# The projection stage with eight ticks of lead and TensorE's work in halves

## The chip, the core and the metric

The kernel runs on one core of one Trainium2 chip. TensorE multiplies matrices into PSUM, VectorE, ScalarE and GpSimd compute elementwise and scan, and SyncE issues every DMA here. The metric is the device time of one execution in microseconds, the median of several runs.

## What is computed

Four layers over a batch of four 64 x 64 images of 96 channels. The first two are state-space layers: group norm, an input projection to 2 x 192 channels, a depthwise convolution, then four scans (k = 0 to 3) over the 4096 pixels in four orders, with 16 states a channel. The change touches what follows a scan. In the reference's words, cut:

```
y = y1 + y2 + y3 + y4                      # the four directions; D * u is in them
mu, var = y.mean(-1), y.var(-1)            # over 192 channels
y = (y - mu) * rsqrt(var + 1e-05) * ln_w + ln_b
y = y * silu(z)
return y @ out_proj_w.T                    # 192 -> 96, added to x
```

Layers three and four are linear attention and a feed-forward network in a low-precision format, on the same images.

## The kernel before

**The scan.** Eight scans (4 images x 2 layers) of 16 windows of 24 steps, 3072 steps. In a step, TensorE fills two PSUM banks with B by a selection matmul (`fill`, L988), VectorE multiplies them by delta*u (L1501) and scans 128 x 1024 states (L1516); in two steps of eight GpSimd forms that product (L1601) and VectorE only scans (L1512). ScalarE gives the decay (L1255), GpSimd multiplies the states by C (L1593) and TensorE sums them (`reduce2`, L1001). `fill(n + 1)` waits for scan n - 1, since it writes over its bank. The loads of a window are SyncE's: a group of four 512 KB loads (`dtr`, `dur`, L697 and L702) at each of steps 0, 8 and 18, C and B (L682, L687) at steps 19, 21, 23 and 1.

**Side stages.** All else runs beside the scan as generators in `pre` (norm and convolution), `post` (sums, norm, gate, projection) and `attn`. Every engine steps its own copy twice a step: a tick. A window has 48 ticks, and a scan's first 15 windows have 720. A stage says at which tick each engine does what; engines wait for one another by semaphores alone. `LEAD` yields 14 ticks before the first stage of a scan, `X_LEAD` 8 ticks before a stage that loads x. The post of scan s runs in scan s + 1; the last one, post 7, has no scan beside it and runs in a tail with the last two attention layers.

**`post`.** It takes eight chunks of 512 pixels, the 192 channels as two halves h of 96. Beside a scan a chunk starts every 39 ticks (`POST_EVERY`), in the tail every 13 (`POST_LANES`); s is a chunk's own tick. TensorE sums four directions and D*u in PSUM at s = 0, 2, 4, 8, 10 (L836; the loads are `sd<-y_d` and `sd<-u_d`, the fourth and fifth given at s = 3 and 5), ScalarE copies (L1114), TensorE centres (L846, L847), ScalarE copies and squares (L1118, L1119), TensorE sums the squares (L852), ScalarE takes the root (L1122, L1124), VectorE multiplies (L1426), ScalarE applies weight and bias (L1128), GpSimd multiplies by z (L1559), TensorE projects (L857) and VectorE adds to x (L1431). In the tail VectorE forms the sum itself (L1412 to L1421), and three lanes of buffers let chunks overlap. An fp32 matmul stands in the profile as two records.

In layer 0 two of the four directions are read with a stride (8 floats in a row), in layer 1 all are contiguous. Posts 0, 1, 4, 5 are of layer 0; 2, 3, 6, 7 of layer 1.

Of the kernel before, what the change touches and what calls it, by code (L numbers as in the profile page):

```python
# [238 lines left out]
def build_program(nc, a, out):  # L239
# [17 lines left out]
    with ctx:  # L257
# [217 lines left out]

        def post_every(overlapped):
            return POST_EVERY if overlapped else POST_LANES
# [7 lines left out]
        def post_ticks(overlapped):  # L485
            return post_every(overlapped) * (C8 - 1) + 39
# [20 lines left out]
        def _(sp):  # L507
# [82 lines left out]
            def post(j, overlapped):  # L590
# [174 lines left out]
        def _(pe):  # L765
# [48 lines left out]
            def post(j, overlapped):  # L814
                b, l = order[j]
                done = before["post", j]
                side_banks(done)
                if not overlapped:
                    pe.wait_ge(scan_v, W * NT)
                for tick in range(post_ticks(overlapped)):  # L820
                    for c in range(C8):
                        s = tick - post_every(overlapped) * c
                        m = C8 * done.post + c
                        bank = lane(c, overlapped).bank
                        if overlapped and s in SUM_AT:
                            i = SUM_AT.index(s)
                            k = SUMS[i]
                            buf, arrived, n = sum_buffer(m, 5 * c + i, overlapped)
                            pe.wait_ge(arrived, n)
                            if i == 0:  # L830
                                after(pe, px_v, through(m, c, overlapped))
                            for h in range(2):
                                v = buf[:, h, :]
                                if l == 0 and k in (1, 3):
                                    v = v.rearrange("p (w r) -> p r w", r=ROWS)
                                mm = pe.matmul(ps[0:CH, bank + h, :], eye[:, :] if k < K else dg[:, l, h, :], v,  # L836
                                               start=(i == 0), stop=(i == K))
                            mm.then_inc(sm_p, 1)
                        if s == 15:
                            if overlapped:  # L840
                                pe.wait_ge(ys_a, m + 1)
                            else:
                                pe.wait_ge(yt_v, c + 1)
                                after(pe, px_v, through(m, c, overlapped))
                            for h in range(2):
                                pe.matmul(ps[0:CH, bank + h, :], cen[:, :], lane(c, overlapped).ys[:, h, :], start=True, stop=False)  # L846
                                mm = pe.matmul(ps[0:CH, bank + h, :], crs[:, :], lane(c, overlapped).ys[:, 1 - h, :], start=False, stop=True)  # L847
                            mm.then_inc(ct_p, 1)
                        if s == 20:
                            pe.wait_ge(xc_a, m + 1)  # L850
                            for h in range(2):
                                mm = pe.matmul(ps[0:CH, bank, :], o192[:, :], lane(c, overlapped).zq[:, h, :], start=(h == 0), stop=(h == 1))  # L852
                            mm.then_inc(pv_p, 1)
                        if s == 35:
                            pe.wait_ge(pg_g, m + 1)
                            for h in range(2):
                                mm = pe.matmul(ps[0:CH, bank + 1, :], wo[:, l, h, :], lane(c, overlapped).ys[:, h, :], start=(h == 0), stop=(h == 1))  # L857
                            mm.then_inc(pj_p, 1)
                    yield
# [196 lines left out]
        def _(act):  # L1056
# [46 lines left out]
            def post(j, overlapped):  # L1103
                b, l = order[j]
                N = before["post", j].post
                for tick in range(post_ticks(overlapped)):
                    for c in range(C8):
# [3 lines left out]
                        if overlapped and s == 12:  # L1111
# [3 lines left out]
                        if s == 17:  # L1115
# [4 lines left out]
                        if s == 22:  # L1120
# [4 lines left out]
                        if s == 26:  # L1125
# [212 lines left out]
        def _(dve):  # L1338
# [60 lines left out]
            def post(j, overlapped):  # L1399
                N = before["post", j].post  # L1400
                for tick in range(post_ticks(overlapped)):
                    for c in range(C8):
# [19 lines left out]
                        if s == 24:  # L1422
# [5 lines left out]
                        if s == 37:  # L1428
# [110 lines left out]
        def _(pool):  # L1539
# [10 lines left out]
            def post(j, overlapped):  # L1550
                N = before["post", j].post
                for tick in range(post_ticks(overlapped)):
                    for c in range(C8):
                        if tick - post_every(overlapped) * c == 27:
# [151 lines left out]
```

## Time and profile before

| | |
|---|---|
| median of 3 runs | 12069.41 us (12066.87 to 12089.06) |
| the profiled execution | 12060.41 us, its span 12058.5 us |
| TensorE, VectorE, ScalarE, GpSimd busy | 74%, 84%, 59%, 81% |
| mean granted TensorE clock | 0.726 of 2.4 GHz |
| DMA | 1630 MB, mean 135 GB/s |
| issue to landing, `dtr`, `dur`, `sd<-y_d` (median) | 8.0, 8.6, 5.1 us |

The span is from the first to the last instruction. Busy time of an engine leaves out issuing and waiting. In the timeline a row is a run of equal instructions of one engine; what stands in brackets is the idle time of the engine just before it and who ended it. SPq is SyncE's queue: its time in a row is that of issuing, which grows when the queues are full.

### The profile page before, as it was taken

To read this page: it belongs to the slowest core of one execution; us is meant where nothing else is said; L and a number is where in the kernel's file an instruction comes from. 1 tells how busy PE (TensorE), PEld (TensorE's weight loads), DVE (VectorE), ACT (ScalarE), POOL (GpSimd) and SP (SyncE) were. 2 spreads that over 40 slices of the span, in tenths; PEclk is the share of its full clock that TensorE was granted. 3 is DMA by queue.
4 is the path that set the end of the run, shared out by engine and by line. 5 is a ranking of instruction groups with operands and counts; after the bars stand their busy time and mean duration, and the time that the engine had idled before them with its cause. 6 is when DMAs were issued, how large, how long until landed. Compare 5 with 4: busy or idle time off the path is not lost.

```text
span 12058.5 us, 94250 instructions
## 1 busy us (share of the span) xinstructions
PE 8904.7 (74%) x26272; PEld 2246.7 (19%) x26272; DVE 10157.8 (84%) x6020; ACT 7059.9 (59%) x10794; POOL 9743.3 (81%) x4231
## 2 busy tenths in 40 slices
PE   6876677876779667778777777787677976777746
PEld 2211111211112111212112121122111221121112
DVE  3899988899889988889888897898888888888841
ACT  4665555664556555576556765566655665557726
POOL 3799988888888988888888887888888888888830
PEclk8875566865779567778677776787677976777756
DMA  4666688566776566556675668766677656655530
GB/s 98 138 140 127 132 145 147 141 133 135 147 146 147 133 142 162 135 124 153 151 165 131 126 147 147 143 142 137 132 148 150 142 131 153 146 142 125 122 97 6
DMA packets 1781576, 1630.40 MB, mean 135 GB/s; under 512 B 1323950, under 2 KB 1325264, under 8 KB 1781052
## 3 DMA queue, kind: packets, MB, share of 16 engines
q1 hardware_dynamic: 1781052, 1624.37, 62.0%
q8 instruction: 212, 3.47, 0.1%
q14 instruction: 312, 2.56, 0.1%
HBM read 624.25 MB, written 194.51 MB: 68 GB/s over the span
## 4 chain that ended last, share of the span: by engine, by line
issue 24%; POOL 19%; DVE 19%; PE 19%; ACT 8%; SPq 6%; DMA 5%; DVEq 0%; POOLq 0%; ACTq 0%
POOL pr L1593 12%; DVE ps L1501 8%; DVE hs L1516 8%; POOL dur L1601 4%; PE ps L836 3%; PE ps L1001 3%; SPq L702 3%; PE ps L805 3%; POOL us L1584 2%; DVE hs L1512 2%; PE ps L988 2%; ACT dec L1255 2%; DMA sd<-y_d 1%; PE ps L963 1%; PE ps L979 1%
## 5 line engine op out<-in xcount | busy, mean ns | idle before, releaser
L1593 POOL TENSOR_TENSOR pr<-hs,crep 128x1024 f32<-128x1024 f32 x3072 | 7190.3, 2353 | 1506.3 <-DVE hs L1516 956.4
L1516 DVE TENSOR_TENSOR_SCAN hs<-dec,carry,ps 128x1024 f32<-128x1024 f32 x1728 | 4054.2, 2346 | 233.8 <-ACT dec L1255 10.3
L988 PE MATMUL ps<-sbc,selb 96*128 96x512 bf16 x4608 | 1859.3, 496 | 2013.1 <-DVE hs L1516 1292.4
L1501 DVE TENSOR_TENSOR ps<-ps,dur 128x1024 f32<-128x1024 f32 x2304 | 2788.6, 1210 | 556.2 <-PE ps L988 420.1
L1255 ACT ACTIVATE dec<-dtr,ac 128x1024 f32<-128x1024 f32 x2304 | 2611.2, 1136 | 372.1 <-DVE hs L1516 371.6
L1001 PE MATMUL ps<-pr,red 128*32 128x512 f32 x12288 | 2290.0, 828 | 79.7 <-POOL pr L1593 73.8
L1262 ACT ACTIVATE carry<-hs 128x1 f32<-128x1 f32 x2304 | 457.3, 199 | 2688.8 <-DVE hs L1516 2311.4
L1601 POOL TENSOR_TENSOR dur<-dur,brep 128x1024 f32<-128x1024 f32 x768 | 1805.9, 2351 | 124.1 <-DMA brep<-bc_d 110.4
L1512 DVE TENSOR_TENSOR_SCAN hs<-ps,carry,dur 128x1024 f32<-128x1024 f32 x576 | 1342.4, 2337 | 330.3 <-POOL dur L1601 247.9
L1516 DVE TENSOR_TENSOR_SCAN hs<-dec,zero,ps 128x1024 f32<-128x1024 f32 x576 | 1351.2, 2346 | 82.2 <-ACT dec L1255 11.0
L805 PE MATMUL ps<-xb,tapw 96*96 96x512 f32 x2304 | 1200.1, 643 | 37.9 <-ACT sd L1091 35.5
L988 PEld LDWEIGHTS ps<-sbc,selb 96*128 96x128 bf16 x4608 | 368.9, 108 | 4198.6 <-DVE hs L1516 2382.8
L1255 ACT ACTIVATE ps<-dtr,ac 128x1024 f32<-128x1024 f32 x768 | 848.3, 1105 | 390.2 <-DVE hs L1516 390.1
L979 PE MATMUL ps<-xdf,tapw 6*96 6x512 f32 x1024 | 770.9, 842 | 62.4 <-ACT sbc L1222 34.7
L963 PE MATMUL ps<-us,xp 96*102 96x512 f32 x1024 | 690.8, 812 | 107.1 <-ACT us L1208 77.9
L836 PE MATMUL ps<-sd,eye 96*96 96x512 f32 x896 | 646.5, 854 | 166.9 <-DMA sd<-y_d 166.8
L1584 POOL TENSOR_TENSOR us<-us,de 96x1024 f32<-96x1024 f32 x256 | 603.3, 2357 | 159.0 <-ACT de L1239 159.0
L1512 DVE TENSOR_TENSOR_SCAN hs<-ps,zero,dur 128x1024 f32<-128x1024 f32 x192 | 447.9, 2338 | 124.4 <-POOL dur L1601 112.9
L1001 PEld LDWEIGHTS ps<-pr,red 128*32 128x32 f32 x12288 | 277.6, 125 | 1235.3 <-issue 939.9
L805 PEld LDWEIGHTS ps<-xb,tapw 96*96 96x96 f32 x2304 | 359.0, 170 | 768.7 <-issue 692.9
L1222 ACT ACTIVATE sbc<-ps 96x512 bf16<-96x512 f32 x768 | 443.9, 578 | 23.1 <-PE ps L969 22.9
L1208 ACT ACTIVATE us<-ust 96x128 f32<-96x128 f32 (+3 forms) x608 | 350.1, 652 | 90.1 <-DMA ust<-u_d 90.1
(220 smaller groups left out, 6883.4 us busy)
## 6 DMA issues: line engine op xcount, KB each, us to landing
dtr<-de SPq DMA_DIRECT2D x768, 512.0 KB, 8.0
dur<-us SPq DMA_DIRECT2D x768, 512.0 KB, 8.6
crep<-bc_d SPq DMA_DIRECT2D x512, 512.0 KB, 5.4
ust<-u_d SPq DMA_DIRECT2D x256, 384.0 KB, 6.7
y_d<-yst SPq DMA_DIRECT2D x768, 128.0 KB, 4.4
sd<-y_d SPq DMA_DIRECT2D x448, 192.0 KB, 5.1
brep<-bc_d SPq DMA_DIRECT2D x128, 512.0 KB, 5.8
u_d<-sd SPq DMA_DIRECT2D x64, 384.0 KB, 3.1
```

Of the source, the lines that this page charges most:

```text
L805: mm = pe.matmul(bank, tap[:, l, t, h * CH:(h + 1) * CH], xb[:, c * ROWS + t // 3:c * ROWS + t // 3 + ROWS, t % 3:t % 3 + SIDE], start=(t ...
L836: mm = pe.matmul(ps[0:CH, bank + h, :], eye[:, :] if k < K else dg[:, l, h, :], v, start=(i == 0), stop=(i == K))
L979: pe.matmul(ps[0:CH, PB, :], dtw[:, order[s][1], k, h * CH:(h + 1) * CH], xdf[XD:XROWS, :], start=True, stop=True, tile_position=(XD, 0)). ...
L988: mm = pe.matmul(ps[:, SLOT + 2 * (n % RS) + hf, :], selb[:, i % GT // 2, :], sbc[:, w % 2, B * hf:B * (hf + 1)], start=True, stop=True)
L1001: mm = pe.matmul(ps[32 * strip:32 * strip + 32, YB, :], red[:, :], pr[:, (2 * m + j) % RP, B * hf:B * (hf + 1)], start=(q == 0), stop=(q = ...
L1255: act.activation(to, dtr[:, 2 * (G % 2) + i % 2, :], ACT.Exp, scale=ac[:, order[s][1], k, i:i + 1]).then_inc(exp_a, 1)
L1501: dve.tensor_tensor(slot(n), slot(n), dur[:, 2 * (G % 2) + i % 2, :], ALU.mult).then_inc(bu_v, 1)
L1512: dve.tensor_tensor_scan(hs[:, n % RH, :], slot(n), dur[:, 2 * (G % 2) + i % 2, :], init, ALU.mult, ALU.add).then_inc(scan_v, 1)
L1516: dve.tensor_tensor_scan(hs[:, n % RH, :], dec[:, others(n) % RD, :], slot(n), init, ALU.mult, ALU.add).then_inc(scan_v, 1)
L1584: pool.tensor_tensor(v, v, de[:, half(h, w), :], ALU.mult).then_inc(du_g, 1)
L1593: pool.tensor_tensor(pr[:, n % RP, :], hs[:, n % RH, :], crep[:, q, :], ALU.mult).then_inc(prod_g, 1)
L1601: pool.tensor_tensor(v, v, brep[:, :], ALU.mult).then_inc(bup_g, 1)
```

## The change

Beside a scan, `post` yields eight more ticks on every engine: SyncE after the first six half tiles of y and the load of x, the others before anything. TensorE's sums, which stood with both halves in one tick, stand in two following ticks; the centring in s = 15 and 17, the sum of squares in 21 and 22, the projection in 35 and 36. The other engines' ticks move by one or two. The ticks of the chunk also move in the tail, where there is no lead.

```diff
+        def post_lead(overlapped):
+            return X_LEAD if overlapped else 0
...
                 load_x(done, a["x"][b] if l == 0 else x_d[b])
+                for _ in range(post_lead(overlapped)):
+                    yield
...
-                        if s == 22:
+                        if s == 23:
                             sp.wait_ge(pv_p, m + 1)
...
-                        if overlapped and s in SUM_AT:
-                            i = SUM_AT.index(s)
+                        at = s - s % 2
+                        h = s % 2
+                        if overlapped and at in SUM_AT:
+                            i = SUM_AT.index(at)
...
-                            for h in range(2):
-                                v = buf[:, h, :]
...
-                            mm.then_inc(sm_p, 1)
-                        if s == 15:
...
+                            if h == 1:
+                                mm.then_inc(sm_p, 1)
+                        if s in (15, 17):
+                            h = (s - 15) // 2
+                            if h == 0 and overlapped:
                                 pe.wait_ge(ys_a, m + 1)
...
-                            for h in range(2):
-                                pe.matmul(ps[0:CH, bank + h, :], cen[:, :], lane(c, overlapped).ys[:, h, :], start=True, stop=False)
-                                mm = pe.matmul(ps[0:CH, bank + h, :], crs[:, :], lane(c, overlapped).ys[:, 1 - h, :], start=False, stop=True)
-                            mm.then_inc(ct_p, 1)
-                        if s == 20:
...
+                        if s in (21, 22):
+                            h = s - 21
...
-                        if s == 35:
...
+                        if s in (35, 36):
+                            h = s - 35
```

ScalarE's ticks 12, 17, 22, 26 become 13, 19, 24, 28; VectorE's 24 and 37 become 26 and 38; GpSimd's 27 becomes 29. SyncE's 3, 5, 12, 14, 31 and 38 and VectorE's 11 (the sums of the tail) stay.

VectorE in the tail, from behind its first sum: before. L1412, L1413, L1416 and L1421 are the sum of a chunk, L1426 the multiply, L1431 the residual.

```order
L1426 TENSOR_TENSOR sd<-sd,ps 96x512 x2
L1412 TENSOR_TENSOR dec<-dec,us 96x1024
L1413 TENSOR_TENSOR us<-us 96x1024
L1416 SCALAR_TENSOR_TENSOR hs<-hs,dsum,us 96x512 x2
L1421 TENSOR_TENSOR pr<-dec,hs 96x1024
L1431 TENSOR_TENSOR xb<-xb,ps 96x8x64
L1426 TENSOR_TENSOR pr<-pr,ps 96x512 x2
L1412 TENSOR_TENSOR hs<-hs 96x1024
L1413 TENSOR_TENSOR dec<-dec 96x1024
L1416 SCALAR_TENSOR_TENSOR dec<-dec,dsum 96x512 x2
L1421 TENSOR_TENSOR crep<-hs,dec 96x1024
L1431 TENSOR_TENSOR xb<-xb,ps 96x8x64
```

The same place after the change (L1431, L1432, L1435 and L1440 are the sum, L1445 the multiply, L1450 the residual):

```order
L1431 TENSOR_TENSOR dec<-dec,us 96x1024
L1432 TENSOR_TENSOR us<-us 96x1024
L1435 SCALAR_TENSOR_TENSOR hs<-hs,dsum,us 96x512 x2
L1440 TENSOR_TENSOR pr<-dec,hs 96x1024
L1445 TENSOR_TENSOR sd<-sd,ps 96x512 x2
L1431 TENSOR_TENSOR hs<-hs 96x1024
L1432 TENSOR_TENSOR dec<-dec 96x1024
L1435 SCALAR_TENSOR_TENSOR dec<-dec,dsum 96x512 x2
L1440 TENSOR_TENSOR crep<-hs,dec 96x1024
L1450 TENSOR_TENSOR xb<-xb,ps 96x8x64
L1445 TENSOR_TENSOR pr<-pr,ps 96x512 x2
L1431 TENSOR_TENSOR us<-us 96x1024
```

The sum of the next chunk stood behind the multiply of the chunk before it; now it stands ahead of the multiply, and ahead of the residual too where there is one.

TensorE in the tail, the centring of chunk 2 and what follows it: before. `cen` and `crs` are centring, `o` the sum of squares, `wo` the projection.

```order
L846 MATMUL ps<-pr,cen 96x512
L847 MATMUL ps<-pr,crs 96x512
L846 MATMUL ps<-pr,cen 96x512
L847 MATMUL ps<-pr,crs 96x512
L852 MATMUL ps<-pr,o 96x512 x2
L857 MATMUL ps<-sd,wo 96x512 x2
L846 MATMUL ps<-crep,cen 96x512
L847 MATMUL ps<-crep,crs 96x512
L846 MATMUL ps<-crep,cen 96x512
L847 MATMUL ps<-crep,crs 96x512
L852 MATMUL ps<-crep,o 96x512 x2
```

After the change (L856 and L857 centring, L864 the sum of squares, L871 the projection):

```order
L856 MATMUL ps<-pr,cen 96x512
L857 MATMUL ps<-pr,crs 96x512
L856 MATMUL ps<-pr,cen 96x512
L857 MATMUL ps<-pr,crs 96x512
L864 MATMUL ps<-pr,o 96x512
L871 MATMUL ps<-sd,wo 96x512
L864 MATMUL ps<-pr,o 96x512
L871 MATMUL ps<-sd,wo 96x512
L856 MATMUL ps<-crep,cen 96x512
L857 MATMUL ps<-crep,crs 96x512
L856 MATMUL ps<-crep,cen 96x512
```

Both halves of the squares stood ahead of the projection of the chunk before; now the two alternate, a half each.

TensorE beside the scan, the first chunk of post 0, from the end of its sums: before. `selb` are fills, `red` reductions, `xp`, `neg` and `xdf` the scan's preparation.

```order
L1001 MATMUL ps<-pr,red 32x512 x4
L836 MATMUL ps<-sd,dg 96x512 x2
L979 MATMUL ps<-xdf,tapw 96x512
L1001 MATMUL ps<-pr,red 32x512 x4
L846 MATMUL ps<-sd,cen 96x512
L847 MATMUL ps<-sd,crs 96x512
L846 MATMUL ps<-sd,cen 96x512
L847 MATMUL ps<-sd,crs 96x512
L988 MATMUL ps<-sbc,selb 128x512 x2
L979 MATMUL ps<-xdf,tapw 96x512
L988 MATMUL ps<-sbc,selb 128x512 x2
```

After the change, from the first half of the centring:

```order
L1003 MATMUL ps<-sbc,selb 128x512 x4
L1016 MATMUL ps<-pr,red 32x512 x4
L856 MATMUL ps<-sd,cen 96x512
L857 MATMUL ps<-sd,crs 96x512
L1003 MATMUL ps<-sbc,selb 128x512 x2
L856 MATMUL ps<-sd,cen 96x512
L857 MATMUL ps<-sd,crs 96x512
L1003 MATMUL ps<-sbc,selb 128x512 x2
L1016 MATMUL ps<-pr,red 32x512 x4
L978 MATMUL ps<-us,xp 102x512 x2
L864 MATMUL ps<-sd,o 96x512
```

The eight records of centring stood together between two fills; each half has its own place now, and so has each half of the squares.

SyncE's queue from the first loads of post 0: before. `dtr` and `dur` are group 2 of the window.

```order
L588 DMA sd<-y_d 96x64x8 x4
L588 DMA sd<-y_d 96x512 x2
L549 DMA xb<-in_x 96x64x64
L697 DMA dtr<-de 128x1x1024 x2
L702 DMA dur<-us 128x1x1024 x2
L588 DMA sd<-y_d 96x512 x2
L588 DMA sd<-u_d 96x512 x2
L677 DMA bc_d<-xdf 32x512
L710 DMA y_d<-yst 64x512 x2
```

After the change:

```order
L591 DMA sd<-y_d 96x64x8 x4
L591 DMA sd<-y_d 96x512 x2
L552 DMA xb<-in_x 96x64x64
L702 DMA dtr<-de 128x1x1024 x2
L707 DMA dur<-us 128x1x1024 x2
L682 DMA bc_d<-xdf 32x512
L715 DMA y_d<-yst 64x512 x2
L591 DMA sd<-y_d 96x512 x2
L591 DMA sd<-u_d 96x512 x2
```

The fourth and fifth load (the `y_d` and `u_d` pairs behind `dur`) stood ahead of the copy `bc_d` and the store of y; now they stand behind both.

## Rows read from the trace of the kernel before

**Rows 1.** The page's costliest groups, VectorE's scan and multiply: busy, mean ns, idle before, releaser.

```profile
L1516 DVE TENSOR_TENSOR_SCAN hs<-dec,carry,ps 128x1024 f32<-128x1024 f32 x1728 | 4054.2, 2346 | 233.8 <-ACT dec L1255 10.3
...
L1501 DVE TENSOR_TENSOR ps<-ps,dur 128x1024 f32<-128x1024 f32 x2304 | 2788.6, 1210 | 556.2 <-PE ps L988 420.1
```

**Rows 2.** Table by stretch: PE, PEld, DVE, ACT, POOL busy (x); PEclk, DMA share, GB/s.

```profile
2532.00:2892.00 360.00, 235.92 (x672) 38.76 (x664) 338.15 (x187) 189.11 (x269) 330.32 (x144) 0.54 0.66 135
11563.00:11755.00 192.00, 102.28 (x129) 31.52 (x130) 66.20 (x64) 37.42 (x48) 21.77 (x8) 0.63 0.36 94
```

**Rows 3.** Waits over the span: who, for whom, us, times, longest.

```profile
DVE ps L1501 <- PE ps L988: 420.1, 214, 12.2
...
PE ps L836 <- DMA sd<-y_d: 166.8, 32, 13.2
...
DVE xb L1431 <- PE ps L857: 133.7, 29, 15.1
```

**Rows 4.** Timeline of post 2, first chunk: start, us, engine, line, then idle before it.

```profile
4399.68 6.22 SPq L702 DMA_DIRECT2D dur<-us  x2
...
4412.49 3.73 PE L836 MATMUL ps<-sd,eye 96*96 96x512 f32 x4 [9.86 <-DMA sd<-y_d]
...
4417.11 1.23 DVE L1501 TENSOR_TENSOR ps<-ps,dur 128x1024 f32<-128x1024 f32 x1 [8.15 <-PE ps L988]
```

**Rows 5.** Groups of VectorE in the first chunk of post 0.

```profile
L1501 DVE TENSOR_TENSOR ps<-ps,dur 128x1024 f32<-128x1024 f32 x16 | 19.5, 1216 | 17.1 <-PE ps L988 17.1
```

**Rows 6.** Groups of VectorE in the first chunk of post 2.

```profile
L1501 DVE TENSOR_TENSOR ps<-ps,dur 128x1024 f32<-128x1024 f32 x16 | 19.4, 1211 | 9.0 <-PE ps L988 9.0
```

**Rows 7.** Waits of VectorE in chunks 1 to 4 of post 0.

```profile
DVE ps L1501 <- PE ps L988: 13.1, 7, 3.8
```

**Rows 8.** Timeline of post 0, last chunk, VectorE behind the fourth sum.

```profile
2135.57 1.23 DVE L1501 TENSOR_TENSOR ps<-ps,dur 128x1024 f32<-128x1024 f32 x1 [7.21 <-PE ps L988]
```

**Rows 9.** Timeline of SyncE's queue at the group loads of step 8.

```profile
1864.45 6.45 SPq L702 DMA_DIRECT2D dur<-us  x2
```

**Rows 10.** Timeline of post 0, third chunk, the sum of u.

```profile
1743.71 3.73 PE L836 MATMUL ps<-sd,dg 96*96 96x512 f32 x4 [3.75 <-DMA sd<-u_d]
```

**Rows 11.** Waits of VectorE in attention 0, second phase, from tick 21 of a window.

```profile
DVE xb L1479 <- PE ps L921: 2.7, 3, 1.0
```

**Rows 12.** Waits of VectorE in attention 1, second phase, from tick 29 of a window.

```profile
DVE xb L1479 <- PE ps L921: 11.3, 3, 8.3
```

**Rows 13.** Timeline of one round of the tail's post.

```profile
11652.50 2.84 POOL L1559 TENSOR_TENSOR sd<-sd 96x1024 f32<-96x1024 f32 x1 [20.67 <-ACT sd L1128]
11653.17 3.37 DVE L1416 SCALAR_TENSOR_TENSOR us<-us,dsum,dec 96x512 f32<-96x512 f32 x2
...
11657.86 2.02 PE L846 MATMUL ps<-pr,cen 96*96 96x512 f32 x2 [8.91 <-DVE pr L1421]
...
11662.68 1.02 PE L847 MATMUL ps<-pr,crs 96*96 96x512 f32 x2
...
11665.72 3.73 PE L852 MATMUL ps<-pr,o 96*96 96x512 f32 x4 [2.02 <-ACT pr L1119]
...
11669.24 3.50 PE L857 MATMUL ps<-sd,wo 96*96 96x512 f32 x4
...
11673.39 1.27 DVE L1426 TENSOR_TENSOR pr<-pr,ps 96x512 f32<-96x512 f32 x2
...
11681.65 2.02 PE L846 MATMUL ps<-crep,cen 96*96 96x512 f32 x2 [8.90 <-DVE crep L1421]
```

**Rows 14.** The tail's two additions with a factor, by name: min/median/max ns.

```profile
L1416 DVE SCALAR_TENSOR_TENSOR dec<-dec,dsum,hs x4: 739/745/2709, 11565.8 to 11727.4; 96x512 f32<-96x512 f32 x4
```

**Rows 15.** Timeline of post 0, first chunk, gate and projection.

```profile
1637.44 2.34 POOL L1559 TENSOR_TENSOR sd<-sd 96x1024 f32<-96x1024 f32 x1
...
1644.02 3.73 PE L857 MATMUL ps<-sd,wo 96*96 96x512 f32 x4
```

More of the change, by code:

```diff
@@ L816, in post @@
                 done = before["post", j]
+                for _ in range(post_lead(overlapped)):
+                    yield
                 side_banks(done)
@@ L839, in post @@
-                        if s == 15:
-                            if overlapped:
+                            if h == 0:
+                                pe.wait_ge(arrived, n)
+                                if i == 0:
+                                    after(pe, px_v, through(m, c, overlapped))
+                            v = buf[:, h, :]
+                            if l == 0 and k in (1, 3):
+                                v = v.rearrange("p (w r) -> p r w", r=ROWS)
+                            mm = pe.matmul(ps[0:CH, bank + h, :], eye[:, :] if k < K else dg[:, l, h, :], v,
+                                           start=(i == 0), stop=(i == K))
@@ L848, in post @@
-                            mm.then_inc(ct_p, 1)
-                        if s == 20:
[L850 to L853, printed above, removed]
-                        if s == 35:
[L855 to L858, printed above, removed]
+                            pe.matmul(ps[0:CH, bank + h, :], cen[:, :], lane(c, overlapped).ys[:, h, :], start=True, stop=False)
@@ new lines, in post @@
+                            mm = pe.matmul(ps[0:CH, bank + h, :], crs[:, :], lane(c, overlapped).ys[:, 1 - h, :], start=False, stop=True)
+                            if h == 1:
+                                mm.then_inc(ct_p, 1)
+                        if s in (21, 22):
+                            h = s - 21
+                            if h == 0:
+                                pe.wait_ge(xc_a, m + 1)
+                            mm = pe.matmul(ps[0:CH, bank, :], o192[:, :], lane(c, overlapped).zq[:, h, :], start=(h == 0), stop=(h == 1))
+                            if h == 1:
+                                mm.then_inc(pv_p, 1)
@@ L859, in post @@
+                        if s in (35, 36):
+                            h = s - 35
+                            if h == 0:
+                                pe.wait_ge(pg_g, m + 1)
+                            mm = pe.matmul(ps[0:CH, bank + 1, :], wo[:, l, h, :], lane(c, overlapped).ys[:, h, :], start=(h == 0), stop=(h == 1))
+                            if h == 1:
+                                mm.then_inc(pj_p, 1)
                     yield
@@ L1105, in post @@
                 N = before["post", j].post
+                for _ in range(post_lead(overlapped)):
+                    yield
                 for tick in range(post_ticks(overlapped)):
@@ L1110, in post @@
                         v = lane(c, overlapped)
-                        if overlapped and s == 12:
+                        if overlapped and s == 13:
                             act.wait_ge(sm_p, 5 * m + 5)
@@ L1400, in post @@
                 N = before["post", j].post
+                for _ in range(post_lead(overlapped)):
+                    yield
                 for tick in range(post_ticks(overlapped)):
@@ L1551, in post @@
                 N = before["post", j].post
+                for _ in range(post_lead(overlapped)):
+                    yield
                 for tick in range(post_ticks(overlapped)):
                     for c in range(C8):
-                        if tick - post_every(overlapped) * c == 27:
+                        if tick - post_every(overlapped) * c == 29:
                             m = C8 * N + c
```

19 lines of the change are left out of this document (6 added, 13 removed).

## Prediction

> **What bounds the kernel now.** I read the page's busy shares first (VectorE leads with 84%), then its costliest groups, a table by stretch, the waits, and the timeline of single chunks. In a step of the scan VectorE multiplies (1.21 us) and scans (2.35 us), 3.56 us [rows 1]; in two of eight steps it only scans, so eight steps are 26.2 us, 3.27 each. Where no side stage runs, 107 steps take 360 us, 3.37 each [rows 2]: there VectorE is the bound and little is to be had. What can be had is its idle time beside side stages. The largest wait of VectorE is for TensorE's fill, 420.1 us, and the residual addition's wait for the projection is 133.7 us. TensorE's sums themselves waited 166.8 us for y loads, 32 times [rows 3].
>
> TensorE is in order. In step n its fill for step n+1 waits for scan n-1, then come a reduction (every second step) and two ticks of side work. A fill must be ready about 3.6 us after it could have begun, and whatever stands before it beyond that stops VectorE. So I ask of each side instruction what the next fill waits for.
>
> **1. The eight ticks of lead.** The three sums of the first chunk whose loads come first don't wait long. The fourth does: in post 2 TensorE stood 9.86 us for `sd<-y_d`, and VectorE 8.15 us behind it [rows 4]. SyncE had come late to that load: its `dur` issue before it took 6.22 us, with the 1.5 MB of x in the queues. Over its first chunk VectorE waited for fills 17.1 us in post 0 and 9.0 us in post 2 [rows 5, 6]; over the four middle chunks of post 0 it was 13.1 us, 3.3 a chunk [rows 7]. Posts 0, 1, 4, 5 (first layer, strided loads) are like post 0 and 2, 3, 6 like post 2. With the lead TensorE wants the fourth load at tick 30 instead of 22, four steps or 14 us later; SyncE gives it in step 12 and no longer ahead of the y store, and some 3 us later. If the chunk then costs a middle chunk's wait: 4 x 13.8 + 3 x 5.7 = 72 us.
>
> The lead also moves every chunk against the 48 ticks of a window. Chunks began at ticks 14, 5, 44, 35, 26, 17, 8, 47 of a window, and will at 22, 13, 4, 43, 34, 25, 16, 7. Seven of the new places are the old ones less one tick, a chunk later; 47 goes and 22 comes.
> - The chunk at 47 gives its fourth load right behind the group loads of a new window: VectorE waited 7.21 us in post 0 [rows 8]. It recurs at the same step of each post; I take 6.4 us each, 45 us gained. The place 22 has its loads between two groups of loads.
> - The second chunk stands at 13, and its fourth load right behind the loads of group 2. There the group's last pair, `dur`, took 6.45 us to issue [rows 9], and the fourth load stands behind it; TensorE wants it after 2.5 steps (9 us), and it has to issue and land in what is left. I put 5 us on VectorE in each post, 35 us lost.
> - The chunk at 44 waited 3.75 us for u [rows 10]. At 43 the first half of that sum falls a step earlier, before another fill: 2 us each, 15 us lost.
> - What follows the post moves four steps. The second phase of attention waited 2.7 us where it began at tick 21 of a window, and 11.3 us at tick 29, where it meets the next group of loads [rows 11, 12]. By these two, three places go from the cheap one to the dear one and two leave a middling one: 14 us lost net.
>
> Sum of part 1: 72 + 45 - 35 - 15 - 14 = 53 us gained. Bounds: 130 if the second chunk's and u's wait don't come, 0 if the first chunk's wait stays at half.
>
> **2. The halves beside the scan.** Nothing is added; every matmul is still there. A pair of ticks starts a step in even chunks, so there the two halves of a sum still stand together, as before; in odd chunks they part. Since the chunks that were even become odd, each place keeps about what it had or is thinner. The centring parts in all chunks: at 1.2 GHz its eight records took 5.84 us in the tail (11657.86 to 11663.70, [rows 13]), which with a fill and a reduction is past the 3.6 + 3.6 us that two fills allow; in halves it isn't. The middle chunks lose 3.3 us each to fills [rows 7], of which sums at 1.2 GHz are the larger part: a sum in both halves is 3.73 us there [rows 4]. I take a tenth of the 420.1 us minus the waits of part 1, some 25 us; bounds 0 and 100 (a third of all that isn't a wait for a load). The residual's wait was 133.7 us, of which 111 us are the tail's; the rest, 22 us in 21 waits of up to 1.9 us, falls where both halves of the projection stood one tick pair ahead. It parts too: 8 us gained (bounds 0 and 22).
>
> **3. Tighter hand-overs.** The gate on GpSimd comes two ticks later against TensorE's projection. Gate end to projection was 1639.78 to 1644.02, 4.2 us, in the first chunk of post 0 [rows 15]. A step less leaves 0.6 there. TensorE will wait here and there for a microsecond, mostly inside the 3.6 us of slack: 5 us lost (bounds 0 and 170, the rival below). SyncE's z load waits for TensorE one tick later, and GpSimd for z one tick later: even.
>
> Parts 1 to 3: 53 + 25 + 8 - 5 = 81 us gained.
>
> **4. The post of the tail, outside the scan.** Here tick numbers alone set the order, and it changes for good. A round of one chunk was 23.79 us (TensorE's centring 11657.86 to 11681.65, [rows 13]), and it was one serial loop: centring 5.84 us, ScalarE 2.02, variance 3.73, projection of the chunk before 3.50 (its end releases the residual), residual and multiply of VectorE 1.9 (from the projection's end at 11672.74), its additions 7 us, of which 3.37 are two that take 0.74 each when GpSimd is still and up to 2.71 beside it [rows 13, 14], then centring. Residual, multiply and additions stood in one tick, additions last. Now the additions of the next chunk stand before the residual and the multiply, so they run beside TensorE's centring of this one, and the loop falls apart in two. TensorE's: 5.84 + 2.02 + 3.73 + 3.50 = 15.1 us at the clock of now, and half of all but ScalarE's part at 2.4 GHz, 2.02 + 6.5 = 8.5 us. VectorE's: 7 + 1.9 = 8.9 us. The gate isn't in the way: after the variance come two steps of ScalarE, the multiply and the affine step, 4 us by my estimate, and the gate's 2.84 us [rows 13], 7 us together, while TensorE does centring, waits and half a variance (9 to 10 us). The stretch ran at a granted clock of 0.63 with TensorE busy 102 of 192 us [rows 2]. A round is thus between 8.9 and 15.1; I take 13, nearer the cold end, since the clock was low there. Loads come as before, ten of 192 KB a round, and had time. Six rounds (chunk 1 to 7) gain 6 x 10.8 = 65 us, and the second chunk no longer waits for the first one's multiply, 5 us: 70 us. Bounds 57 and 94.
>
> The Trainium skill (SBUF — State Buffer, "Who interferes with whom") says that a VectorE instruction with two SBUF inputs and a GpSimd instruction that reads SBUF lock each other out. The trace agrees: the two additions at 11653.17 take 3.37 us beside the gate at 11652.50 [rows 13]. By that rule the additions keep their 2 us of blocking in the new order; the 7 us above have them in.
>
> **Sum.** 81 + 70 = 151 us. The profiled execution took 12060.4 us, so 11909; the median of the three runs is 9 us above it: 11918. A difference under 0.2% (24 us) can't be told from none.
>
> **Rivals.**
> - *Only the tail gains.* The waits for loads are those of a full queue at each group of loads, and the shift finds as many new collisions as it leaves; parts 1 to 3 come to nothing. For it: 47 and 14 are the two worst places, but I know 22 and 13 only by neighbours. Against: the x load stays at tick 14 while the fourth load moves away from it. Time: 12069 - 70 = 11999.
> - *The clock goes up and the second chunk doesn't wait.* Denser work in the tail keeps TensorE at 2.4 GHz, with rounds of 10.5 us: 6 x 13.3 + 5 = 85 us; beside the scan the 35 us of the second chunk stay away: 116 us. 12069 - 201 = 11868. For it: the granted clock was 0.54 where TensorE had fills, reductions and preparation only [rows 2], and it is 0.73 over all, so more work went with a higher clock. The Trainium skill (TensorE: Matmul & The Clock Gate, "What's actually happening") says that activity releases the throttle; by it the tail gains and the thinner work beside the scan may lose.
> - *TensorE waits for the gate.* At the projection the slack of 4.2 us [rows 15] shrinks by a step, and GpSimd is behind whenever VectorE is. If the gate comes one GpSimd instruction (2.35 us) later than in the rows, TensorE waits up to 4 us in 40 of 56 chunks with the next fill behind it, and VectorE loses some 4 us each, 170 us. It decides from 1.5 us a chunk. Time: 12069 - 86 (parts 1 and 2) - 70 + 170 + what SyncE's wait for the gate at tick 31 delays, one group load of 1.3 us in each chunk, 73 = 12156. Against: a z that lands late holds VectorE too, so TensorE isn't early.
> - *The lead doesn't do what it says*: SyncE is late by its queues, not by its tick, and the first chunk's fourth load is late again after store and copy. Half of the 72 us is lost: 11954; it lies in the forecast's own range.
>
> **Chances.** Forecast (11850 to 11965) 0.55; only the tail 0.22; the clock up 0.13; the gate 0.05; nothing to be told 0.05. Range 11850 to 12015. Faster by over 0.2%: 0.90; same 0.05; slower 0.05.
>
> **What would show it.** The tail's centrings 13 us apart, VectorE's additions beside them, and the post there 70 us shorter. TensorE's longest waits for `sd<-y_d` in first and last chunks gone, a new one of some 5 us in the second. VectorE's wait for the fill from 420 to about 320 us, for the projection from 134 to under 60. The second phase of attention at some 11 us in the third scan. Wrong would be: rounds of 20 us or more in the tail, or TensorE waiting for GpSimd at the projection by over 50 us in total.

## The result, and the profile after

The changed kernel took 11886.66 us (median of 4, 11876.67 to 11915.99) against 12068.14 us before (4 runs): ratio 0.9858 (of the means), 95% interval 0.9826 to 0.9889. That is 181 us faster by the medians and 172 by the means, with the interval from 134 to 210; the forecast was 151 us and 11918. Its profiled execution has a span of 11877.7 us, 180.8 less than before, so the two traces can be compared part by part.

The page's costliest groups after, in the form of [rows 1] (L1535 is the scan, L1520 the multiply, L1003 the fill):

```profile
L1535 DVE TENSOR_TENSOR_SCAN hs<-dec,carry,ps 128x1024 f32<-128x1024 f32 x1728 | 4054.5, 2346 | 234.6 <-POOL pr L1614 7.2
L1520 DVE TENSOR_TENSOR ps<-ps,dur 128x1024 f32<-128x1024 f32 x2304 | 2787.8, 1210 | 432.7 <-PE ps L1003 281.1
```

The busy time of both is the same to a microsecond; the idle time before the multiply fell from 556.2 to 432.7 us. The waits after, as in [rows 3] (L845 are TensorE's sums, L1450 the residual, L871 the projection, L1622 GpSimd's product with `brep`):

```profile
DVE ps L1520 <- PE ps L1003: 281.1, 187, 6.6
...
POOL dur L1622 <- DMA brep<-bc_d: 194.2, 50, 15.2
...
PE ps L845 <- DMA sd<-y_d: 78.0, 29, 6.1
...
PE ps L845 <- DMA sd<-u_d: 44.7, 10, 7.6
PE ps L871 <- POOL sd L1580: 44.2, 7, 13.3
DVE xb L1450 <- PE ps L871: 31.9, 15, 10.5
```

VectorE's wait for the fill fell by 139 us and the residual's by 102. Three waits rose: TensorE's for u (17.0 us before) and for the gate (1.0 before), and GpSimd's for `brep`, the B rows for its products, which was

```profile
POOL dur L1601 <- DMA brep<-bc_d: 110.4, 40, 13.3
```

before. With it VectorE's wait for GpSimd's product rose from 360.8 to 381.3 us.

**By place.** The last scan ended 104.8 us earlier on the span, 9.5 of it in the first scan, where nothing was changed; the tail is 76.0 us shorter. To see what a chunk costs beside the scan I took, in each trace, the time between the ends of the scans at which it and the next chunk start (halfway between two ends where a chunk starts in mid-step). A place is the tick of the window at which a chunk starts. Means of the four posts of layer 0 and the three of layer 1, us:

| chunk | 0 | 1 | 2 | 3 | 4 | 5 | 6 | 7 | sum |
|---|---|---|---|---|---|---|---|---|---|
| place before | 14 | 5 | 44 | 35 | 26 | 17 | 8 | 47 | |
| layer 0 | 88.0 | 71.4 | 73.8 | 82.8 | 80.9 | 70.4 | 73.5 | 75.9 | 616.7 |
| layer 1 | 76.0 | 71.3 | 72.1 | 74.2 | 68.3 | 70.1 | 72.4 | 76.2 | 580.7 |
| place after | 22 | 13 | 4 | 43 | 34 | 25 | 16 | 7 | |
| layer 0 | 77.8 | 70.5 | 70.8 | 75.9 | 83.9 | 81.1 | 70.0 | 72.3 | 602.4 |
| layer 1 | 67.8 | 69.8 | 70.8 | 77.9 | 72.8 | 69.2 | 70.0 | 70.5 | 568.8 |

The sums give 4 x 14.3 + 3 x 11.9 = 93 us. Read along the places, not the chunks: in layer 0, 35 and 34, 26 and 25, 17 and 16 cost nearly the same, one chunk later. Over all seven posts the first chunk fell by 9.4 us each (66 us), and place 13 costs 5.8 us less than place 47, for which it came (41 us); place 43 costs 3.7 us more than 44 (26 us lost). Such sums move between executions of the same code: in e3 below, whose code beside the scan is that of the changed kernel, all seven posts together take 17 us less.

The first chunk of post 2 after, VectorE's multiply, as in [rows 6], and that of post 0, as in [rows 5]:

```profile
L1520 DVE TENSOR_TENSOR ps<-ps,dur 128x1024 f32<-128x1024 f32 x15 | 18.1, 1206 | 0.0
```

```profile
L1520 DVE TENSOR_TENSOR ps<-ps,dur 128x1024 f32<-128x1024 f32 x15 | 18.2, 1212 | 7.9 <-PE ps L1003 4.0 <-DMA dur<-us 3.9
```

In layer 1 the wait is gone. In post 0 the wait for the fill fell from 17.1 to 4.0 us, and one of 3.9 us for `dur` came: the timeline of post 0 shows that the scan's own group 2 is now behind x and the strided loads.

```profile
1566.15 0.58 SPq L552 DMA_DIRECT2D xb<-in_x  x1
...
1566.87 9.48 SPq L702 DMA_DIRECT2D dtr<-de  x2
...
1576.39 6.38 SPq L707 DMA_DIRECT2D dur<-us  x2
...
1587.83 1.23 DVE L1520 TENSOR_TENSOR ps<-ps,dur 128x1024 f32<-128x1024 f32 x1 [3.90 <-DMA dur<-us]
```

**The tail.** A table row of the tail's post, as the second of [rows 2], and its timeline, as [rows 13] (L856, L857 centring, L1431 and L1435 additions):

```profile
11475.00:11575.00 100.00, 74.09 (x117) 24.17 (x118) 56.71 (x59) 35.25 (x46) 18.73 (x8) 0.74 0.51 145
```

```profile
11516.63 1.10 PE L856 MATMUL ps<-pr,cen 96*96 96x512 f32 x2
11516.64 0.69 DVE L1450 TENSOR_TENSOR xb<-xb,ps 96x512 f32<-96x512 f32 x1
11517.24 1.27 DVE L1445 TENSOR_TENSOR sd<-sd,ps 96x512 f32<-96x512 f32 x2
...
11519.28 1.02 PE L857 MATMUL ps<-pr,crs 96*96 96x512 f32 x2
...
11522.33 1.95 PE L864 MATMUL ps<-pr,o 96*96 96x512 f32 x2 [2.02 <-ACT pr L1136]
11522.44 1.22 DVE L1431 TENSOR_TENSOR us<-us 96x1024 f32<-96x1024 f32 x1 [3.92 <-DMA hs<-u_d]
...
11529.19 1.07 PE L856 MATMUL ps<-crep,cen 96*96 96x512 f32 x2
```

From centring to centring it is 12.6 us here and 11.9 on the mean of six rounds (centrings of chunks 1 to 7, 11479.9 to 11551.2), where the mean was 23.6. VectorE's additions now wait for a load and not for TensorE, and TensorE is busy 74% of the time at a granted clock of 0.74 (before: 53% at 0.63).

### The profile page after: what moved, and what is told of

Its sections match the earlier page's. It is cut to its first block, busy times and chain, and to the rows that moved or that the text cites. A ratio compares the mean times of both kernels' runs of the same rounds, so it can differ in the third digit from the quotient of the medians.

```text
span 11877.7 us, 94251 instructions
## 1 busy us (share of the span) xinstructions
PE 8881.1 (75%) x26272; PEld 2213.0 (19%) x26272; DVE 10149.7 (85%) x6020; ACT 7067.1 (59%) x10794; POOL 9744.5 (82%) x4231
## 4 chain that ended last, share of the span: by engine, by line
issue 25%; POOL 20%; DVE 19%; PE 17%; ACT 7%; SPq 7%; DMA 5%; DVEq 0%; POOLq 0%; ACTq 0%
POOL pr L1614 12%; DVE ps L1520 8%; DVE hs L1535 8%; POOL dur L1622 4%; SPq L707 3%; PE ps L1016 3%; PE ps L845 3%; POOL us L1605 2%; DVE hs L1531 2%; PE ps L1003 2%; PE ps L810 2%; PE ps L994 1%; ACT dec L1272 1%; PE ps L978 1%; DMA brep<-bc_d 1%
## 5 line engine op out<-in xcount | busy, mean ns | idle before, releaser
L1535 DVE TENSOR_TENSOR_SCAN hs<-dec,carry,ps 128x1024 f32<-128x1024 f32 x1728 | 4054.5, 2346 | 234.6 <-POOL pr L1614 7.2
L1003 PE MATMUL ps<-sbc,selb 96*128 96x512 bf16 x4608 | 1852.8, 494 | 2034.2 <-DVE hs L1535 1278.5
L1520 DVE TENSOR_TENSOR ps<-ps,dur 128x1024 f32<-128x1024 f32 x2304 | 2787.8, 1210 | 432.7 <-PE ps L1003 281.1
L1622 POOL TENSOR_TENSOR dur<-dur,brep 128x1024 f32<-128x1024 f32 x768 | 1808.1, 2354 | 255.9 <-DMA brep<-bc_d 194.2
L1535 DVE TENSOR_TENSOR_SCAN hs<-dec,zero,ps 128x1024 f32<-128x1024 f32 x576 | 1351.4, 2346 | 81.3 <-ACT dec L1272 11.2
L1003 PEld LDWEIGHTS ps<-sbc,selb 96*128 96x128 bf16 x4608 | 371.0, 108 | 4213.7 <-DVE hs L1535 2425.4
L845 PE MATMUL ps<-sd,eye 96*96 96x512 f32 x896 | 632.6, 826 | 80.3 <-DMA sd<-y_d 78.0
```

What stands on the lines that cost most here:

```text
L1003: mm = pe.matmul(ps[:, SLOT + 2 * (n % RS) + hf, :], selb[:, i % GT // 2, :], sbc[:, w % 2, B * hf:B * (hf + 1)], start=True, stop=True)
L1520: dve.tensor_tensor(slot(n), slot(n), dur[:, 2 * (G % 2) + i % 2, :], ALU.mult).then_inc(bu_v, 1)
L1535: dve.tensor_tensor_scan(hs[:, n % RH, :], dec[:, others(n) % RD, :], slot(n), init, ALU.mult, ALU.add).then_inc(scan_v, 1)
L1622: pool.tensor_tensor(v, v, brep[:, :], ALU.mult).then_inc(bup_g, 1)
```

## Experiments

Each ran on the chip beside the kernel before, and all but one in five rounds. Ratios are to it. Chunk times are means as in the table above.

**e1: the lead alone**, on the kernel before.

```diff
+        def post_lead(overlapped):
+            return X_LEAD if overlapped else 0
... (in post, on each engine)
+                for _ in range(post_lead(overlapped)):
+                    yield
```

> The kernel before with the eight ticks of lead alone; no halves, all ticks of a chunk as before, the tail as before. The prediction's part 1 made this 53 us, with 35 us lost in the second chunks (their fourth load behind the group loads); the changed kernel shows no such wait there. Theory A (the lead and the shift of places do it alone): first chunks of layer-0 posts fall from 88 to about 78 us, the chunk at place 47 (75.9 us) goes, the second chunk at place 13 stays at 70 to 71 us; 60 to 85 us gained in all, 11983 to 12008. Rival (the halves keep the second chunk quick): with whole sums and a whole centring the second chunk costs 75 us or more, 7 x 5 us, and the gain is 30 to 50 us, 12018 to 12038.

Measured 11979.18 us, 0.9926 (0.9914 to 0.9938): 91 us, just past the upper end of theory A, whose first chunks came too: 77.4 in layer 0, 68.5 in layer 1. But the second chunk stands at 74.9 and 73.8, against 70.5 and 69.8 with the halves, and the fourth at 79.8 and 79.0, against 75.9 and 77.9. That is the rival's slow second chunk, without its small gain. VectorE in the second chunk of post 2, with the lead alone:

```profile
DVE ps L1512 <- PE ps L995: 4.5, 1, 4.5
DVE xb L1442 <- PE ps L864: 2.1, 1, 2.1
```

and with the halves, where TensorE still waits for the fourth load:

```profile
PE ps L845 <- DMA sd<-y_d: 6.1, 1, 6.1
...
DVE ps L1520 <- PE ps L1003: 3.5, 1, 3.5
```

So the wait that I had put on place 13 exists in both. Over the seven second chunks TensorE waits 26.7 us for y loads in e1 and 27.0 with the halves. What the halves take away there is VectorE's wait for the projection (13.6 us over the seven in e1, none with the halves) and a quarter of its wait for the fill (34.5 to 25.7).

**e2: no lead**, the changed kernel with `post_lead` returning 0.

> The changed kernel without the lead: halves and moved ticks everywhere. The prediction's parts 2 and 3 and the tail: 28 + 76 us (the tail as the changed kernel's trace has it), 11964, first chunk again with a wait of 7 to 13 us for the fourth load. Rival (the halves are the gain beside the scan and the lead only moves waits about): 11887 to 11910. Other rival (halves come to nothing beside the scan): 11992.

Measured 11926.1 us, 0.9885 (0.9872 to 0.9898): 144 us, between the first two figures. The tail is 84 us shorter in its trace. The first chunk is again 87.4 and 74.8 us. The halves and ticks gave about 50 us beside the scan (a last scan that ends 54 us earlier on the span), not 28.

**e3: the old tail**, the changed kernel with all old ticks where no scan runs.

> The changed kernel with the old order in the tail (all ticks of a chunk as before where no scan runs, both halves together). Theory: beside the scan nothing changes, the tail's post has rounds of 23.8 us again and is 76 us longer: 11963. Rival (part of the tail's 76 us is a higher clock carried over or a shorter attention tail): less than 60 us back.

Measured 11979.62 us, 0.9918 (0.9905 to 0.9932): above the changed kernel by 93 us by medians and 72 by the two ratios; the profiled spans differ by 76.7. Rounds of 23.7 us are back. The profiled execution (span 11954.4) is one of e3's quickest, so I don't lean on its chunk times. The medians of e1 and e3 are equal, and by the ratios e3 is 10 us faster with intervals of some 15 us to each side of both: on top of the lead, the halves beside the scan are worth nothing that can be measured, though alone they gave 50.

**e4: one number in the tail**, on the kernel before: VectorE's multiply.

```diff
-                        if s == 24:
+                        if s == (24 if overlapped else 26):
```

> The kernel before with one number changed: in the tail VectorE's multiply stands at tick 26 instead of 24, behind the additions of the next chunk. Theory (prediction, part 4): the serial loop breaks there, TensorE's halves have nothing to do with it; rounds of 12 to 15 us instead of 23.8, 55 to 75 us gained, 11993 to 12013. Rival (the halves are needed, since variance and projection stand whole between two centrings): rounds above 17 us, under 45 us gained, over 12023.

Measured 12047.33 us, 0.9981 (0.9972 to 0.999): 23 us. The theory's figures fell and the rival's came (rounds above 17 us, over 12023), though not for its reason, as e5 shows; rounds are 20.4 us. The timeline says why:

```profile
11642.34 3.42 PE L857 MATMUL ps<-crep,wo 96*96 96x512 f32 x4
...
11645.80 0.68 DVE L1431 TENSOR_TENSOR xb<-xb,ps 96x512 f32<-96x512 f32 x1 [13.54 <-PE ps L857]
11646.40 1.22 DVE L1412 TENSOR_TENSOR hs<-hs,dec 96x1024 f32<-96x1024 f32 x1
...
11651.50 2.02 PE L846 MATMUL ps<-pr,cen 96*96 96x512 f32 x2 [5.75 <-DVE pr L1421]
```

VectorE stood 13.54 us at the residual with the additions behind it: the residual still shared a tick with them and stood first.

**e5: both numbers in the tail**, e4 and the residual at 38.

```diff
-                        if s == 37:
+                        if s == (37 if overlapped else 38):
```

> The kernel before with two numbers changed, in the tail alone: VectorE's multiply at tick 26 instead of 24 and its residual at 38 instead of 37, each behind the additions of a later chunk. The multiply alone left rounds of 20.4 us, since the residual still stood ahead of the additions. Theory: the residual carries the other half of the loop, and VectorE's order alone gives the tail's gain: rounds of 12 to 14 us, 60 to 76 us gained, 11994 to 12010. Rival (TensorE's order, variance whole ahead of the projection, is needed too): rounds of 16 us or more.

Measured 11988.77 us, 0.9934 (0.9921 to 0.9946): 78 us. With TensorE's code as before, the rounds are 11.9 us:

```profile
11642.72 1.02 PE L846 MATMUL ps<-pr,cen 96*96 96x512 f32 x2
11642.92 0.69 DVE L1431 TENSOR_TENSOR xb<-xb,ps 96x512 f32<-96x512 f32 x1 [1.48 <-PE ps L857]
...
11646.14 1.22 DVE L1412 TENSOR_TENSOR us<-us 96x1024 f32<-96x1024 f32 x1 [1.35 <-DMA hs<-u_d]
...
11653.54 1.02 PE L846 MATMUL ps<-crep,cen 96*96 96x512 f32 x2
```

Its trace has the tail 83 us shorter, the changed kernel's 76. The tail's gain is the order of VectorE's additions, multiply and residual; the halves add nothing to it.

**e6: the multiply back at 24 in the tail**, all else as changed (3 rounds).

> The changed kernel with VectorE's multiply back at tick 24 in the tail, ahead of the additions of the next chunk; halves and residual as changed. Theory: the multiply closes a loop centring, ScalarE, variance, ScalarE, multiply, additions, about 21 us a round; 50 to 65 us lost against the changed kernel, 11937 to 11952. Rival (TensorE's halves free the order): rounds of 12 to 15 us and no loss.

Measured 11964.24 us, 0.9922 (0.9906 to 0.9937): 78 us lost; rounds of 22.8 us. By the traces 63 of it are in the tail, as expected; the last scan also ended 20 us later, where the code is the same, and that is spread between executions. Either of the two numbers, left as it was, keeps most of the loop.

**e7: x later**, the changed kernel with x at tick 6 of the first chunk.

```diff
-                load_x(done, a["x"][b] if l == 0 else x_d[b])
+                if not overlapped:
+                    load_x(done, a["x"][b] if l == 0 else x_d[b])
...
+                    if overlapped and tick == 6:
+                        load_x(done, a["x"][b] if l == 0 else x_d[b])
```

> The changed kernel with the load of x (1.5 MB) at tick 6 of the first chunk instead of ahead of the lead. The changed kernel's trace has group 2 of the first window late in layer-0 posts: its first issue takes 8.82 us behind x, its dur lands 12 us after, and VectorE waits 3.9 to 5.9 us for it and 4 us in the next step. Theory: x fills the queues there; without it layer-0 first chunks fall from 78 to 70 us, 4 x 8 = 32 us gained beside nothing lost, 11855. Rival (the strided loads of y fill the queues, x is harmless): same as the changed kernel, 11887. Other rival (x collides with the next group at step 18): slower, above 11900.

Measured 11876.73 us, 0.9847 (0.9834 to 0.986): 10 us below the changed kernel, not the 32 expected, and the spread doesn't tell it from nothing. Layer-0 first chunks fell from 77.8 to 73.4, second chunks rose from 70.5 to 73.4. The wait for `dur` was x's, as I thought, and x took it along to the next group.

**e8: brep first**, the changed kernel with SyncE's load of `brep` ahead of group 1.

```diff
                     if i == 0:
+                        load_b(w)
                         load_group(1, w)
                     if i == 1:
-                        load_b(w)
```

> The changed kernel with the load of brep (the B rows for GpSimd's products) ahead of group 1 at step 0 of each window instead of behind it at step 1. GpSimd waits 194 us for it in 50 places, most of them in chunks 4 and 5 of layer-0 posts, 9 to 15 us each. Theory: the load stands behind 2 MB of group loads that nothing needs for eight steps; ahead of them it comes in time and 60 to 100 us are gained, 11787 to 11827. Rival (its landing is bound by the queue of strided loads, not by its place; group 1 is then late in turn): within 20 us of 11887.

Measured 11781.2 us, 0.9763 (0.9749 to 0.9776): 105 us below the changed kernel, just past the theory's upper end. The wait for `brep` in this run:

```profile
POOL dur L1622 <- DMA brep<-bc_d: 3.9, 1, 3.9
```

**e9: brep first on the kernel before.**

> The kernel before with the load of brep ahead of group 1, nothing else. Brep first gained 105 us on the changed kernel. The kernel before waits 110 us for brep in 40 places instead of 194 in 50. Theory (the shift of places had turned part of its gain into waits for brep, which brep first takes away in both): on the kernel before it is worth less, 50 to 80 us, 11987 to 12017, and the change would then be worth 210 to 235 us instead of 181. Rival (worth the same in both): 11962.

Measured 12021.52 us, 0.9951 (0.9936 to 0.9965): 52 us. The same edit is worth twice as much in the changed kernel, so the change had turned some 50 us of its gain into waits for `brep`. With this load out of the way the change is worth 227 (by the ratios) to 240 us (by the medians).

**e10: and u earlier**, e8 with the fifth load at tick 4.

```diff
-                        if overlapped and s in (3, 5):
-                            post_load(j, 5 * c + 3 + (s - 3) // 2, True)
+                        if overlapped and s in (3, 4):
+                            post_load(j, 5 * c + s, True)
```

> The changed kernel with brep first, and the load of u (the fifth of a chunk) at the chunk's tick 4 instead of 5. In the fourth chunk tick 5 is step 0 of a window, where u stands behind group 1: it is issued in step 3 and VectorE waits 4.4 to 7.7 us in step 4 in each of the seven posts. At tick 4 it stands ahead of group 1. Theory: that wait goes, 30 to 40 us, 11741 to 11751. Rival (another load behind u is late instead): 11775 or more.

Measured 11728.1 us, 0.9712 (0.9698 to 0.9726): 53 us below e8, more than expected. The fourth chunk fell from 77.0 and 77.9 us to 70.0 and 67.9. What is left of TensorE's weight loads waiting for u:

```profile
PEld ps L845 <- DMA sd<-u_d: 9.9, 7, 1.7
```

**e11: and x later.**

> The run before with the load of x at tick 6 of the first chunk as well. Alone that gave 10 us: layer-0 first chunks fell by 4.5 us each and the second chunks rose by 3. Expected 10 us below the run before; rival: no difference, or slower by what x now delays (crep and brep of the next window).

Measured 11704.29 us, 0.9695 (0.9681 to 0.9709): 24 us below e10, where 10 were expected. This is the fastest version, 182 us below the changed kernel: three loads given at another place in SyncE's order.

**e12: e11 without any half**, TensorE's work whole and at the old ticks; the lead, e5's two numbers, and the three loads.

> The run before without any half: TensorE's sums, centring, variance and projection whole and at the old ticks, the lead as in the changed kernel, in the tail only VectorE's multiply at 26 and residual at 38; brep first, u at tick 4, x at tick 6. The lead alone and the lead with halves (both with the old tail) came out at 11979.2 and 11979.6 us. Theory A (by these medians: the halves beside the scan are worth nothing once the lead is there): within 15 us of the run before, 11690 to 11720. Theory B (by the traces, where the halves took 4 us off the chunk at place 13 and 3 to 5 off the one at place 43): 20 to 45 us above it, 11725 to 11750.

Measured 11753.5 us, 0.9729 (0.9716 to 0.9742): 49 us slower than e11 by medians, 41 by the ratios. Second chunks are 74.8 and 73.5 us again (71.1 and 69.1 in e11). VectorE's wait for the fill, e12 and e11:

```profile
DVE ps L1515 <- PE ps L998: 315.0, 193, 7.8
```

```profile
DVE ps L1523 <- PE ps L1006: 271.5, 167, 7.7
```

The last scan ends 54 us later than in e11, and the tail's rounds are 11.9 us (11.4 in e11). So theory B, at or just past its upper end: the halves with their ticks are worth 40 to 50 us beside the scan, and in e3 that didn't show. They have a price, VectorE's wait for GpSimd's product: from e12 to e11 it rises from 188.3 to 236.8 us, from e1 to the changed kernel, where `brep` is late, from 285.5 to 381.3. One place where it rises is chunk 5 of post 0, step 0 of a window on. With the lead alone:

```profile
2006.98 1.05 SPq L622 DMA_DIRECT2D sd<-z_d  x2
...
2008.14 1.22 SPq L702 DMA_DIRECT2D dtr<-de  x2
...
2017.74 2.23 SPq L692 DMA_DIRECT2D brep<-bc_d  x1
...
2023.87 2.35 POOL L1614 TENSOR_TENSOR dur<-dur,brep 128x1024 f32<-128x1024 f32 x1 [4.29 <-DMA brep<-bc_d]
```

and with the halves:

```profile
2003.65 2.07 SPq L622 DMA_DIRECT2D sd<-z_d  x2
...
2005.82 1.06 SPq L692 DMA_DIRECT2D brep<-bc_d  x1
...
2011.38 2.34 POOL L1622 TENSOR_TENSOR dur<-dur,brep 128x1024 f32<-128x1024 f32 x1 [7.49 <-DMA brep<-bc_d]
...
2013.85 2.35 DVE L1531 TENSOR_TENSOR_SCAN hs<-ps,carry,dur 128x1024 f32<-128x1024 f32 x1 [5.18 <-POOL dur L1622]
```

The z load's tick went from 22 to 23, and at place 25 that is the step from the end of one window into step 0 of the next: it left its place ahead of group 1 and stood right ahead of `brep`. Layer-0 chunks at place 25 cost 76.7 us in e1 and 81.1 with the halves. Over the span the wait for `brep` was 139.6 us in e1 and 194.2 in the changed kernel. But `brep` isn't what this place costs: with it first the same chunks cost 71.3 us whole (e12) and 75.3 in halves (e11), the same 4 us apart. The z load, now behind group 1, comes late itself; in e8:

```profile
1996.35 4.07 SPq L622 DMA_DIRECT2D sd<-z_d  x2
...
2003.17 2.35 POOL L1580 TENSOR_TENSOR sd<-sd 96x1024 f32<-96x1024 f32 x1 [4.67 <-DMA sd<-z_d]
```

So what ate the halves' gain in e3 stays open. The rise of VectorE's wait for GpSimd is twice as large where `brep` is late, which fits; but e2 has the same 194 us of waits for `brep` and kept its 50, and e11 and e12 differ from e3 and e1 by all three loads. Neither e1 with `brep` first nor z alone at its old tick was run.

## Why the prediction was right, and where it wasn't

The total was forecast at 151 us and measured at 181, inside the range; by the two traces 95 beside the scan (81 forecast) and 76 in the tail (70 forecast), and 10 in stretches that the change doesn't touch, which the spread of the runs covers. The tail's mechanism held. Beside the scan the sum came near in part by luck: the lead alone gave 91 us and the halves alone some 50, each more than forecast, and together they gave 95, since they don't add.

- **Part 1, the lead** (53 us forecast, beside attention's loss 67): e1 gives 94 in its posts. First chunks 65 us, forecast 72: layer 1 lost its wait altogether, layer 0 got the new one for `dur`, which I hadn't named. Place 47 (76.0 us) gone and 13 (74.5) come: 10 us, as forecast (45 - 35). Place 43 for 44: 79.4 against 73.0, 45 us lost, forecast 15, the term that was mis-sized. I had priced half a sum before another fill; what came is the wait for the load of u, given in step 0 behind group 1, which TensorE now wants a tick earlier: 49.8 us over the seven chunks in e1 and 40.6 in the changed kernel, where place 44 had 17.0, and gone in e11 with u at tick 4. The five other places were each taken as unchanged by one tick; by the same count they gave 63 us together (34 for 35: 77.2 against 79.1; 25 for 26: 72.6 against 75.5), which made up for it.
- **Part 2, the halves** (25 + 8): about 50 alone (e2) and 41 to 49 with the loads mended (e12 against e11), more than the 33 of the two terms; with the lead and the old loads nothing that can be measured (e3 against e1). My sentence that odd and even chunks change roles and "each place keeps about what it had" was the weak one: places 13 and 43 are cheaper with the halves (70.2 and 76.7 us in the changed kernel, 74.5 and 79.4 in e1) and place 25 dearer (76.0 against 72.6), so parts 1 and 2 are not a sum of two terms. Which of the halves (sums, centring, squares, projection) does it wasn't run apart; at place 13 the wait that fell most is the residual's for the projection.
- **Part 3** (-5): the step that failed most plainly. "SyncE's z load waits for TensorE one tick later ... even" left out that one tick can carry an issue across a group of loads: place 25 costs 3.4 us more than in e1, and VectorE waits 73 us for GpSimd's product in its seven chunks, 31 in e1. TensorE's wait for the gate came, 44.2 us in 7 waits, one in each chunk at place 25, where GpSimd is late already; with `brep` first it is 20.9 (e8).
- **Part 4, the tail** (70): rounds of 11.9 us against 13 forecast. The mechanism, additions ahead of multiply and residual, is shown by e4, e5 and e6. TensorE's clock rose from 0.63 to 0.74 as its busy share rose, which is the part of the second rival that came true; 11.9 lies about midway between the two bounds, where 13 was taken nearer the cold end. That the loads "had time" held only in part: VectorE's additions now wait 3.92 and 1.88 us for the load of u in the rows shown, though in these rounds TensorE's centring doesn't wait for them.
- **Attention** (-14): its second phase moved as told. In the third post's scan it waited 11.4 us (2.7 before, [rows 11]):

```profile
DVE xb L1498 <- PE ps L936: 11.4, 3, 8.5
```

  and in attention 2, which had waited 8.3, it now waits nothing. Over the six phases beside the scan the idle time rose from 36 to 43 us, so 7 us and not 14.
- **The rivals.** "Only the tail gains" fell by e1 and e2. "The clock goes up and the second chunk doesn't wait" was nearest in time (11868), and that is luck: the clock went up in the tail, but the second chunk does wait, 3.5 us for the fill in post 2, and costs no more than its neighbours all the same. "TensorE waits for the gate" fell.

What also stays open is why the lead alone made places 4, 25, 34 and 7 each some 2 to 3 us cheaper than the ones a tick later; no run moved the places by one tick only.

## What to carry to other kernels

Where several engines step through one table of ticks, ask of each number on which side of the large transfers, and of the other side instruction in the same tick, it puts an instruction: in e4 and e5 two numbers were worth 78 us, and in e8 to e11 three places in a queue were worth 182. Give a queue's loads in the order in which they are needed: `brep`, 512 KB behind 2 MB that nobody needs for eight steps, was late, and moving it ahead gave 105 us. An edit that seems worth nothing on top of another (e3) may be worth something once other waits are gone (e12 against e11), so measure it again there.

## What the runs showed of the hardware

With the same matmuls TensorE's tail stretch ran at a granted clock of 0.63 when it was busy 102 of 192 us [rows 2], and at 0.74 when busy 74 of 100: with waits taken out, many of the matmuls got shorter too. The first pair of centring records takes 1.10 us at 11516.63 and took 2.02 us at 11657.86 [rows 13]; not all do, the pair of squares at 11522.33 still took 1.95. In e5, with TensorE's code as before, 62 us of the tail's rounds stood at 0.81:

```profile
11618.00:11680.00 62.00, 51.90 (x92) 17.73 (x90) 46.58 (x43) 25.07 (x34) 16.43 (x5) 0.81 0.60 172
```

The additions with a factor took 1.41 us in each of the eight rounds after; before, in six of eight, 3.37. What GpSimd's gate now meets, in four rounds of eight, is the first addition:

```profile
11532.94 2.34 POOL L1580 TENSOR_TENSOR pr<-pr 96x1024 f32<-96x1024 f32 x1 [10.45 <-ACT pr L1145]
11533.19 3.17 DVE L1431 TENSOR_TENSOR dec<-dec 96x1024 f32<-96x1024 f32 x1 [1.88 <-DMA us<-u_d]
```

It takes 3.17 us there and 1.22 at 11522.44, where the gate was all but done (it ended at 11522.49). The rule of the Trainium skill (SBUF — State Buffer, "Who interferes with whom") that the two lock each other out is borne out again; the 2 us of blocking moved with the order, as the prediction had it.
